# Four of five sets of identity products left out of the opening of a transformer layer

## What is computed

```python
q, k, v, g = x @ Wq, x @ Wk, x @ Wv, x @ Wg          # 128 -> 128, 128, 256, 256
q, k = rope(q), rope(k)
scores = einsum('bhqd,bhkd,hqk->bhqk', q * DQK ** -0.5, k, decay)
o = einsum('bhqk,bhkd->bhqd', scores, v)
o = o * rsqrt(mean(o * o) + EPS) * g_norm_w
x = layernorm(x + (o * silu(g)) @ Wo)
gate, up = fp4_linear(x, w_gate), fp4_linear(x, w_up) # 128 -> 352; x and w rounded in blocks of 16
x = layernorm(x + fp4_linear(silu(gate) * up, w_down))
```

## Time and profile before

| | |
|---|---|
| Time, median of 3 runs | 134.44 us (134.44 to 134.64) |
| Time of the profiled execution | 134.68 us |
| Its span, first to last instruction | 132.9 us |
| TensorE busy, products | 121.9 us (92%) |
| TensorE busy, weight loads (beside the products) | 86.5 us (65%) |
| VectorE busy | 109.8 us (83%) |
| ScalarE busy | 88.7 us (67%) |
| GpSimd busy | 87.8 us (66%) |
| Identity products (line 301) | 40 instructions, from us 1.9 to 21.6 |

### The profile page before, as it was taken

How to read it: one execution, slowest core, us unless ns; L and a number is a source line. 1 busy time by engine, 2 the same in 40 slices (tenths; PEclk the granted TensorE clock), 3 DMA queues, 4 the chain that set the end, 5 groups by cost and what they waited for, 6 DMA issues and landing times.

```text
span 132.9 us, 5148 instructions
## 1 busy us (share of the span) xinstructions
PE 121.9 (92%) x2072; PEld 86.5 (65%) x2072; DVE 109.8 (83%) x329; ACT 88.7 (67%) x311; POOL 87.8 (66%) x124
## 2 busy tenths in 40 slices
PE   4898789999999999999999999899999899999860
PEld 4764447675676576766666577557686688887650
DVE  1239796789689999999999999799999999999810
ACT  3143465573865849576676759687777787899883
POOL 5012443548859667894956688486949797996781
PEclk9999999999999999999999999999999999999999
DMA  3799991000000000000000000000000000010222
GB/s 91 246 282 358 427 435 69 0 7 7 0 5 0 5 5 0 5 2 5 0 7 0 0 5 2 5 5 0 0 5 5 1 21 0 14 50 20 62 79 79
DMA packets 4791, 7.68 MB, mean 58 GB/s; under 512 B 800, under 2 KB 3872, under 8 KB 4512
## 3 DMA queue, kind: packets, MB, share of 16 engines
q1 hardware_dynamic: 3744, 6.60, 14.2%
q10 hardware_dynamic: 1024, 0.76, 1.8%
HBM read 6.31 MB, written 1.05 MB: 55 GB/s over the span
## 4 chain that ended last, share of the span: by engine, by line
PE 73%; DVE 12%; ACT 4%; issue 4%; DMA 3%; POOL 2%; POOLq 0%; DVEq 0%; ACTq 0%
PE ps L313 9%; PE ps L441 7%; PE ps L307 6%; PE ps L421 6%; PE ps L427 6%; PE ps L330 5%; PE ps L355 4%; PE ps L365 4%; PE ps L341 3%; PE ps L301 3%; PE ps L433 3%; PE ps L386 3%; DMA w_qk<-in_w_qk 3%; DVE probs L728 3%; PE ps L387 2%
## 5 line engine op out<-in xcount | busy, mean ns | idle before, releaser
L860 POOL TENSOR_TENSOR rstd_h<-ms,minus_half 128x8 f32<-128x8 f32 x16 | 26.8, 1674 | 7.6 <-DVE ms L744 7.5
L855 POOL TENSOR_TENSOR qk<-rope 128x256 f32<-128x256 f32 x16 | 11.7, 731 | 11.2 <-DVE rope L722 11.2
L313 PE MATMUL ps<-w_vg,xT_sb 128*128 128x512 f32 x32 | 16.7, 604 | 0.5 <-DVE S L739 0.5
L879 POOL TENSOR_TENSOR xq<-x_ratio,xs 128x128 f32<-128x128 f32 x16 | 7.9, 491 | 11.5 <-DVE x_ratio L657 11.5
L722 DVE TENSOR_TENSOR rope<-ps,tabs_sb 128x512 f32<-128x512 f32 x16 | 11.0, 686 | 5.4 <-PE ps L307 5.2
L441 PE MATMUL ps<-wd_T,hT 128*128 128x128 f32 x96 | 14.1, 283 | 1.3 <-DVE r L758 0.7
L871 POOL TENSOR_TENSOR rstd<-veps,minus_half 128x1 f32<-128x1 f32 x16 | 9.3, 581 | 7.7 <-DVE veps L753 7.7
L887 POOL TENSOR_TENSOR hq<-h_ratio,hs 128x352 f32<-128x352 f32 x16 | 13.1, 816 | 1.7 <-DVE h_ratio L657 1.3
L441 PEld LDWEIGHTS ps<-wd_T,hT 128*128 128x128 f32 x96 | 12.1, 191 | 3.1 <-ACT hT L484 1.5
L421 PE MATMUL ps<-wgu_T,xqT 128*128 128x352 f32 x32 | 13.3, 496 | 0.0
L728 DVE TENSOR_TENSOR probs<-ps,causal 128x512 f32<-128x512 f32 x16 | 11.0, 690 | 2.4 <-PE ps L330 2.0
(11 more groups left out here) (110 smaller groups left out, 349.0 us busy)
## 6 DMA issues: line engine op xcount, KB each, us to landing
tabs_sb<-rope_tables SPq DMA_DIRECT2D x1, 2048.0 KB, 12.4
tabs_sb<-rope_tables SPq DMA_DIRECT2D x1, 1280.0 KB, 8.3
out<-x SPq DMA_DIRECT2D x16, 64.0 KB, 1.5
tabs_sb<-rope_tables SPq DMA_DIRECT2D x1, 512.0 KB, 4.3
xT_sb<-x_transposed SPq DMA_DIRECT2D x1, 512.0 KB, 7.9
xT_sb<-x_transposed SPq DMA_DIRECT2D x1, 320.0 KB, 5.6
tabs_sb<-rope_tables SPq DMA_DIRECT2D x1, 256.0 KB, 4.0
w_vg<-in_w_vg ACTq DMA_DIRECT2D x1, 256.0 KB, 4.4
```

Source lines behind the costliest of these rows:

```text
L313: mm(vg_ps, xT(c), w_vg[:], start=True, stop=True).then_inc(vg_pe, 1)
L855: gp.tensor_tensor(g16(qk[:, c % D, :]), g16(rope[:, c % D, 0, :]), g16(rope[:, c % D, 1, :])[:, :, ::-1, :], ALU.add).then_inc(qk_p, 1)
L860: gp.tensor_tensor(rstd_h[:, c, :], ms[:, c, :], minus_half[:], ALU.pow).then_inc(rms_p, 1)
```

## The change

TensorE's order loses four of its five `warm_up(4)` calls: the one behind `project_qk(0)`, and those behind `transpose_qk(0)`, `transpose_qk(1)` and `transpose_qk(2)`. The first call, at the head of the order, stays. The order of all other steps is the same; since it is wrapped anew, the diff marks all its lines, and only its head is shown. In `scores` a slice gets a name, and in `from_state` a line is broken elsewhere.

```diff
@@ scores(c)
-                        rows = slice(32 * j, 32 * j + 32)
-                        last = mm(sc_ps(j)[CH * a:CH * a + CH, :], kT[rows, c % D, CH * a:CH * a + CH],
+                        rows, keys = slice(32 * j, 32 * j + 32), slice(CH * a, CH * a + CH)
+                        last = mm(sc_ps(j)[keys, :], kT[rows, c % D, keys],
@@ the order of TensorE
-            warm_up(4); project_qk(0); warm_up(4); project_vg(0); transpose_qk(0); warm_up(4); project_qk(1)
-            state_product(0); scores(0); project_vg(1); from_state(0); values(0); state_product(1); project_qk(2)
-            transpose_qk(1); warm_up(4); transpose_o(0); project_vg(2); scores(1); project_vg(3); from_state(1)
-            transpose_y(0); values(1); project_qk(3); transpose_o(1); transpose_qk(2); warm_up(4)
-            transpose_gate_up_weights(); state_product(2); transpose_down_weights(); scores(2); project_vg(4)
+            warm_up(4); project_qk(0); project_vg(0); transpose_qk(0); project_qk(1); state_product(0); scores(0)
+            project_vg(1); from_state(0); values(0); state_product(1); project_qk(2); transpose_qk(1); transpose_o(0)
+            project_vg(2); scores(1); project_vg(3); from_state(1); transpose_y(0); values(1); project_qk(3)
+            transpose_o(1); transpose_qk(2); transpose_gate_up_weights(); state_product(2); transpose_down_weights()
+            scores(2); project_vg(4); out_projection(0); transpose_y(1); project_qk(4); from_state(2)
...
```

More of the change, by code:

```diff
@@ L354, in from_state @@
                         rows = slice(32 * j, 32 * j + 32)
[L355 to L356 removed]
+                        mm(oT_bank(n // 4, a)[32 * slot32:32 * slot32 + 32, :], S[rows, (2 * c + a) % 8, e * DV:(e + 1) * DV],
+                           q_eo[rows, c % D, a, e, :], start=True, stop=False)
             def values(c):
@@ L449, in _ @@
[L449 to L473, removed]
@@ new lines, in _ @@
+            scores(2); project_vg(4); out_projection(0); transpose_y(1); project_qk(4); from_state(2)
+            state_product(3); values(2); project_qk(5); transpose_o(2); transpose_qk(3); out_projection(1)
+            state_product(4); scores(3); project_qk(6); from_state(3); values(3); project_qk(7); transpose_qk(4)
+            transpose_o(3); transpose_y(2); transpose_xq(0); project_vg(5); gate(0); scores(4); out_projection(2)
+            from_state(4); state_product(5); values(4); project_qk(8); transpose_o(4); transpose_qk(5); transpose_y(3)
@@ new lines, in _ @@
+            project_vg(6); transpose_xq(1); up(0); scores(5); out_projection(3); from_state(5); state_product(6)
+            values(5); gate(1); transpose_o(5); transpose_qk(6); transpose_y(4); project_vg(7); project_qk(9)
+            transpose_xq(2); up(1); scores(6); out_projection(4); from_state(6); state_product(7); values(6); gate(2)
+            transpose_o(6); transpose_qk(7); transpose_y(5); project_vg(8); project_qk(10); transpose_xq(3); up(2)
+            scores(7); out_projection(5); from_state(7); state_product(8); values(7); gate(3); transpose_o(7)
@@ new lines, in _ @@
+            transpose_qk(8); transpose_y(6); project_vg(9); project_qk(11); transpose_xq(4); up(3); scores(8)
+            out_projection(6); from_state(8); state_product(9); values(8); gate(4); transpose_qk(9); transpose_o(8)
+            transpose_y(7); project_vg(10); project_qk(12); transpose_xq(5); up(4); scores(9); out_projection(7)
+            from_state(9); state_product(10); values(9); gate(5); transpose_o(9); transpose_qk(10); transpose_y(8)
+            project_vg(11); project_qk(13); up(5); transpose_xq(6); out_projection(8); scores(10); gate(6)
@@ new lines, in _ @@
+            from_state(10); state_product(11); values(10); project_qk(14); transpose_o(10); transpose_qk(11)
+            project_vg(12); transpose_xq(7); transpose_y(9); scores(11); up(6); out_projection(9); from_state(11)
+            state_product(12); values(11); gate(7); transpose_qk(12); transpose_o(11); transpose_y(10); project_vg(13)
+            project_qk(15); up(7); transpose_xq(8); out_projection(10); scores(12); gate(8); from_state(12)
+            values(12); state_product(13); transpose_o(12); transpose_qk(13); transpose_y(11); project_vg(14)
@@ new lines, in _ @@
+            transpose_xq(9); up(8); scores(13); out_projection(11); from_state(13); state_product(14); values(13)
+            gate(9); transpose_o(13); transpose_qk(14); transpose_h(0); transpose_y(12); project_vg(15); up(9)
+            transpose_xq(10); out_projection(12); scores(14); gate(10); state_product(15); from_state(14); values(14)
+            transpose_y(13); down(0); transpose_o(14); transpose_h(1); transpose_qk(15); up(10); out_projection(13)
+            transpose_xq(11); down(1); scores(15); gate(11); up(11); from_state(15); values(15); transpose_y(14)
@@ new lines, in _ @@
+            transpose_o(15); transpose_h(2); transpose_xq(12); out_projection(14); gate(12); transpose_h(3); up(12)
+            down(2); transpose_h(4); transpose_y(15); down(3); transpose_h(5); out_projection(15); down(4)
+            transpose_h(6); transpose_xq(13); down(5); gate(13); transpose_h(7); down(6); up(13); transpose_h(8)
+            transpose_xq(14); down(7); gate(14); transpose_h(9); up(14); down(8); transpose_h(10); transpose_xq(15)
+            down(9); up(15); gate(15); transpose_h(11); down(10); transpose_h(12); down(11); transpose_h(13); down(12)
@@ L481, in _ @@
+            transpose_h(14); down(13); down(14); transpose_h(15); down(15)
         @block.scalar
```

6 lines of the change are left out of this document (removed).

## The result

The changed kernel takes 133.0 us (median of 4 runs, 132.9 to 133.42) where the kernel before takes 134.44 beside it (134.4 to 134.64). The ratio is 0.9896 (95% interval 0.9873 to 0.992), so 1.4 us faster. 132.4 was forecast. The profiled execution took 132.9 us with a span of 131.2; before it was 134.68 and 132.9. Both executions put the gain at 1.7 to 1.8 us, not at 2.07.

What follows compares the result with a forecast made beforehand. TensorE was taken as the busiest engine, nearly gapless behind us 30, with VectorE and loads limiting the opening. Terms 0.42 + 0.76 + 0.89 = 2.07 us off 134.44 gave 132.4 us, range 131.7 to 133.5.

Steps and rivals of the forecast that it cites:

- The path of the opening: Steps up to next_state(2, 0): each removed set followed to the next late load or queue; 2.07 us sooner in all.
- terms of 0.42, 0.76 and 0.89: Gains in us forecast for the removed products behind project_qk(0) and transpose_qk(0) together, behind transpose_qk(1), and behind transpose_qk(2).
- four links of the chain: The four removed sets of identity products, 1.40, 0.89, 0.89 and 0.89 us on the chain that ended last.
- set 2: Identity products behind project_qk(0), 1.40 us in the chain; removal was to end project_vg(0) 0.82 us sooner, then loads take over.
- set 4: Identity products behind transpose_qk(1), ahead of transpose_o(0): removal was to bring 0.76 of 0.89 us, using up VectorE's idle time.
- set 5: Identity products behind transpose_qk(2), ahead of transpose_gate_up_weights(): removal was to bring the full 0.89 us at next_state(2, 0).
- sets 2 and 3: Identity products behind project_qk(0) and transpose_qk(0): 2.29 us off TensorE, but only 0.42 gained at rotate(1), loads taking the rest.
- Whatever reaches us 24 should reach the end: Behind us 30 TensorE has almost no gap, so the opening's gain of 2.07 us should carry through to the end.
- The clock still rises at about 6.6: TensorE's clock in the opening: project_vg(0) keeps TensorE at work, so full speed comes as before; no loss taken.
- rival (b): TensorE's clock rises late, at about us 10, in the opening: 0.5 us dearer, 132.9; chance 0.07.
- set 1: Identity products at the head of TensorE's order, ahead of project_qk(0); they stay, no gain counted.
- rival (c): TensorE's clock falls in the thin stretch from us 7 to 17: 2.7 us dearer, 135.1, slower than before; chance 0.06.

Runs made afterwards that it cites:

- sets 2 and 3 both back: Changed kernel with the identity products behind project_qk(0) and transpose_qk(0) put back; median 133.51 us.
- wide sets: Kernel before, all five sets of identity products kept, each as one product of 512 columns instead of four of 128; 134.69 us, ratio 1.0025.
- set 2 back: Changed kernel with the identity products between project_qk(0) and project_vg(0) put back; median 133.15 us.
- set 5 back: Changed kernel with the identity products behind transpose_qk(2) put back; median 135.51 us, ratio to the kernel before 1.0031.
- set 4 back: Changed kernel with the identity products between transpose_qk(1) and transpose_o(0) put back; median 133.99 us.
- loads issued early: Changed kernel with SyncE issuing the second pieces of x and tables before its wait for the first tables piece; 135.13 us, ratio to before 1.0041.
- the control: The changed kernel, unaltered, run again in another series; median 133.68 us, ratio to the kernel before 0.9933.
- no set: Changed kernel with the remaining first warm_up(4) removed too, so no identity products at all; median 133.58 us.
- 64 instructions behind transpose_qk(0): Changed kernel with 16 small identity products (32x32, 64 columns) added between transpose_qk(0) and project_qk(1); median 133.75 us.

## Why the prediction came out as it did

**The path of the opening** was right step by step: 8.05 for project_qk(1), 9.85 for rotate(1), 14.00 for mean_square(0), 21.15 for next_state(2, 0), against 8.09, 9.95, 14.20 and 21.19. The sum up to there was 2.07 and measured 2.11. Its terms of 0.42, 0.76 and 0.89 came out as 0.52, 0.64 and 0.95, so part of the closeness is errors that cancel. mean_square(0) came 1.38 us earlier and not 1.18, but VectorE's next small step took 0.40 us in place of 0.17, which left 1.16; why it did isn't known. That four links of the chain with 4.07 us give half of it is shown by the single sets: set 2 nothing (21.17 against 21.15), set 4 0.75, set 5 0.95 by the two traces; with sets 2 and 3 both back it is 0.73, of which 0.46 are tables that landed later.

The first term rests on more than the two sets. The loads landed sooner in the changed kernel's profile, though nothing in the change moves them: the weights of q and k let project_qk(0) start 0.62 us earlier, those of v and the gate let project_vg(0) start at 5.18 and not at the 5.71 of the prediction, and the second piece of the tables landed about 0.1 earlier. With wide sets, where project_qk(0) also starts at 3.72, all five sets are there and rotate(1) still starts at 9.88. So how much of the 0.52 is the work of sets 2 and 3, and how much that of loads that happened to land sooner, can't be read from one profile of each kernel; the 0.42 came close partly by luck.

**"Whatever reaches us 24 should reach the end"** is the step that failed, by 0.34 us. Removing 64 instructions is itself a change to every instruction behind them. In every kernel with the same number ahead of the tiles as before, wherever and whatever they were (small products in two places, with or without a set), the rest is 107.73 to 107.75; with other numbers it is 107.87 to 108.61. The long tile moves with the number: tiles 6 and 7 at 80 fewer, 7 and 8 at 64 and 60, 8 and 9 at 48, 9 at 32. It isn't exact: with set 5 or set 2 back (48 fewer) tile 9 is short, with set 5 back the rest is 0.11 less than with set 4 back, which missed the 0.05 expected, and with the loads issued early tile 8 is short.

The traces say more than the tile. Count TensorE's weight loads from the start of the span up to the one that is held up. In the changed kernel (first two rows) and in the kernel before with wide sets (last two) it is 844 in the first long group and 970 in the second, though the groups themselves begin at other counts (columns as in the earlier trace rows; the fourth is the weight loads):

```profile
0.00:50.35 50.35, 44.74 (x842) 28.51 (x844) 39.07 (x111) 29.02 (x96) 28.04 (x44) 1.00 0.36 128
...
0.00:56.51 56.51, 50.84 (x969) 32.70 (x970) 45.05 (x129) 33.34 (x112) 33.25 (x50) 1.00 0.32 114
```

```profile
0.00:52.07 52.07, 47.52 (x844) 29.09 (x844) 38.97 (x111) 29.00 (x96) 28.05 (x44) 1.00 0.35 123
...
0.00:58.24 58.24, 53.62 (x969) 33.27 (x970) 44.91 (x129) 33.29 (x112) 33.28 (x50) 1.00 0.31 111
```

With one product to each load these are places 1688 and 1940 of the stream. Counted so in all profiles, the hold of each of the 15 long groups is at place 1436, 1688, 1940 or 2190, and the two stops outside the scores with set 2 back are at 1190 and 1440. In the four kernels with as many instructions ahead as before, no group of scores of tiles 3 to 9 covers such a place. Three groups of these tiles that cover one are short even so, those just named. So it is shown that the stops have fixed places in the stream, and that the number of instructions ahead decides what stands there; whether a stop is made there, and how long it is, that number does not decide. That the places are where TensorE goes from one block of fetched instructions to the next is inferred. The profile counts 16 transfers of 0.26 MB in all on an instruction queue, 16 KB each:

```profile
q8 instruction: 16, 0.26, 0.9%
```

The Trainium skill, Perfetto Trace Analysis, section on the 4-stage abstract model, says that an instruction has 64 bytes; so a block would be 256 of them, an estimate. The places lie about 250 recorded instructions apart; the count leaves out those that only wait, and the 4080 recorded products and weight loads make 16 such blocks. In the changed kernel the transfers at 51.49 and 57.66 begin 1.3 to 1.4 us after the starts of the groups of tiles 7 and 8. No run here changes the block or its timing by itself. Why such a stop lasts 0.15 to 0.25 us in some places, 0.41 in another (set 2 back) and nothing visible elsewhere stays open.

**"The clock still rises at about 6.6"** held in the first profile (6.2) and not in general. The range took in a later rise as rival (b), at 0.07; five of the 14 profiles rise at us 10.0 or later. In the seven profiles in which more identity products stand between set 1 and project_vg(0) (before, wide, set 2 back, sets 2 and 3 back, and the three with small products behind set 1), the rise came at 5.0 to 7.8. In the seven without them it came twice at 6.2 and 6.8 and five times at 10.0 to 18.3. The times fit in the main: 132.38 to 133.93 in the 26 runs of the five kernels that have them and lack sets 4 and 5, none of which spreads over more than 0.93 us, against spreads of 1.20 in the control, 1.74 with no set, 1.63 with set 5 back and 1.39 with 64 instructions behind transpose_qk(0). Against it, set 4 back lacks them and spreads over 0.43 alone, and the kernel before, which has them, reaches 135.68 in one series and 136.18 with wide sets. Its price at about us 10, where (b) said 0.5, is 0.51 us by the kernel with no set, from the landing of the tables to rotate(1). The control is 0.59 later than the first profile, but its tables landed at 10.38, 0.54 later too, so in that execution the late rise added only 0.06. With set 5 back and a rise at 14.6, next_state(2, 0) stands at 24.00; less the 21.15 of the changed kernel and the set's own 0.95 that is a price of 1.9 us, an estimate, as much as the whole gain. That is the price of rival (c) without its fall: no trace has the clock fall before the last product. So set 2, which is worth nothing on the path, may have been of use in keeping the rise early; the grouping was made after the runs, and no kernel was profiled often enough to show it. How much of this is chance stays open: there is one profile for each kernel but the changed one, and its two differ by 3.8 us.

**The missing 0.6 us** between 132.4 and 133.0: the two profiles differ by 134.68 - 132.90 = 1.78 us, which is the 2.11 of the opening less the 0.34 of the rest. The medians differ by 1.44. The remaining 0.34 us are how the profiled executions stand to their medians, 0.24 above it before and 0.10 below it after; I had taken the gain of a profile off a median as it was. How much of that is a later rise in the runs without a profile can't be read.

On the transposes the traces decide against what the prediction cites from the Trainium skill, TensorE: Matmul & The Clock Gate, section on the PE-mode transpose: at the full clock one takes 273 ns, and with set 5 back, before the rise, the same one takes 0.42 us, both as the identity products do.

```profile
7.31 0.42 PE L319 MATMUL ps<-ident,qk 128*128 128x128 f32 x1
```

## What to carry to other kernels

A busy engine's link in the chain is worth only what the next late thing leaves: follow each removed piece to the load or the queue that takes over. Each of the three terms here came out to about 0.1 us. Read more than one profile where the path begins with loads, since these land some tenths of a microsecond sooner or later by themselves. Then ask what else the removed instructions did. Here their number set which small, closely packed products met a stop of the instruction stream, and as many cheap instructions ahead took all long groups away; and a set that was hidden behind the loads may have kept the clock's rise early.

## What was not expected of the hardware

- A group of 16 instructions of small products takes 0.63 to 0.73 us, not 0.47, where it covers a certain place of TensorE's instruction stream (1436, 1688, 1940, 2190 by the count above), though not each time; two such groups are 0.28 of the 0.34 us that the rest grew by.
- The rise of TensorE's clock varied from us 5.0 to 18.3 of the span over 14 profiles of nearly one program, and by 3.8 us between two of the same kernel (6.2 and 10.0). The clock row of the profile's page shows the full level in the opening, also while products take 421 ns; their durations tell, and the place where the record of the clock begins.
- The second piece of the tables landed between us 9.63 and 10.38 in the 13 profiles in which it was issued as before, 9.84 and 10.38 in the two of the same kernel.
- Small products of 32 rows and 32 columns behind set 1 went with rises at 5.6, 5.7 and 7.8, in the range of those with more full ones there (5.0 to 7.7).
